# One core's audio layer: constants spread by a product, the row split on GpSimd, the last pair by batch, new engine lists

## What is computed

```
h = conv3(x) + conv_b                          # per channel, over tokens
h = h^T @ lin_w^T + lin_b + mean(emb)          # 250 x 128 per batch
h = layernorm(h) * ln_g + ln_b                 # gamma, beta
n = layernorm(h)
S = (n Wq)(n Wk)^T                             # 250 x 250 per batch
c0 = argmin(rowsum(S[0]))                      # from batch 0 alone
h = h + softmax(S / 8) (n Wv), row c0 zeroed
n = layernorm(h)
out = h + gelu(n tril(W1)^T + b1) tril(W2)^T + b2
```

## Time and profile before

| what | us |
|---|---|
| median of 3 executions | 94.94 (94.71 to 95.37) |
| profiled execution, its own time | 94.69 |
| its span in the trace | 92.9 |
| PE busy | 87.2 |
| DVE busy | 74.4 |
| ACT busy | 69.3 |
| POOL busy | 47.8 |

### The profile page before, as it was taken

How to read it: one execution, slowest core, us unless ns; L and a number is a source line. 1 busy time by engine, 2 the same in 40 slices (tenths; PEclk the granted TensorE clock), 3 DMA queues, 4 the chain that set the end, 5 groups by cost and what they waited for, 6 DMA issues and landing times.

```text
span 92.9 us, 2013 instructions
## 1 busy us (share of the span) xinstructions
PE 87.2 (94%) x567; PEld 73.9 (80%) x567; DVE 74.4 (80%) x296; ACT 69.3 (75%) x215; POOL 47.8 (51%) x70
## 2 busy tenths in 40 slices
PE   4999699999999999999999999999999999999940
PEld 1356567789999999999999999999997877787840
DVE  3279997999698998869998895988989688793560
ACT  1666799899999969977889976697758983565200
POOL 7006398676554386539525519703996305791000
PEclk9999999999999999999999999999999999999999
DMA  2896000000000000000000000000000003036565
GB/s 17 213 280 212 0 0 4 4 0 0 7 0 0 0 0 0 7 4 0 0 4 4 0 7 0 0 0 0 0 0 7 0 0 110 0 110 169 162 175 167
DMA packets 3973, 3.86 MB, mean 42 GB/s; under 512 B 429, under 2 KB 3962, under 8 KB 3962
## 3 DMA queue, kind: packets, MB, share of 16 engines
q1 hardware_dynamic: 3610, 3.35, 12.8%
q10 hardware_dynamic: 352, 0.38, 1.5%
HBM read 1.68 MB, written 2.05 MB: 40 GB/s over the span
## 4 chain that ended last, share of the span: by engine, by line
PE 80%; DVE 9%; DMA 5%; issue 1%; SPq 0%; DVEq 0%
PE bank_o L483 15%; PE bank_s L458 15%; PE bank_at L470 8%; PE bank_pv L434 7%; PE bank_pv L443 7%; PE bank_s L518 7%; DMA x_all<-x_dram 5%; PE bank_x L366 4%; PE bank_x L496 4%; PE bank_nt L507 4%; PE bank_pv L507 4%; PE bank_nt L423 4%; DVE hb_all L1078 2%; DVE tap_a L994 1%; DVE xc L1000 1%; PE bank_o L366 1%
## 5 line engine op out<-in xcount | busy, mean ns | idle before, releaser
L483 PE MATMUL bank_o<-pv,at_sb 125*125 125x129 f32 x128 | 16.8, 273 | 0.0
L458 PE MATMUL bank_s<-n1t,pv 128*125 128x250 f32 x64 | 16.1, 374 | 0.0
L483 PEld LDWEIGHTS bank_o<-pv,at_sb 125*125 125x125 f32 x128 | 15.6, 187 | 0.1
L772 ACT ACTIVATE a<-bank_s,neg_max 125x250 f32<-125x250 f32 x32 | 13.4, 482 | 1.0 <-DVE neg_max L1039 1.0
L1039 DVE TENSOR_REDUCE neg_max<-bank_s 125x2 f32<-125x500 f32 x16 | 10.7, 668 | 2.2 <-PE bank_s L458 2.1
L458 PEld LDWEIGHTS bank_s<-n1t,pv 128*125 128x125 f32 x64 | 11.0, 187 | 0.9
L780 ACT ACTIVATE at_sb<-bank_at 125x500 f32<-125x500 f32 x16 | 9.6, 597 | 2.4 <-PE bank_at L470 1.8
L276 POOL TENSOR_TENSOR hb_all<-h_all,rows_sb 125x512 f32<-125x512 f32 x8 | 10.9, 1384 | 0.0
L765 ACT ACTIVATE pv<-bank_pv 128x508 f32<-128x508 f32 x15 | 9.0, 602 | 2.1 <-PE bank_pv L443 2.0
L272 POOL TENSOR_TENSOR h_all<-h_all,rows_sb 125x512 f32<-125x512 f32 x6 | 7.6, 1271 | 5.7 <-DVE h_all L1013 5.7
L1050 DVE SCALAR_TENSOR_TENSOR h_all<-bank_o,rinv_keep,h_all 125x128 f32<-125x128 f32 x32 | 9.8, 346 | 0.6
(11 more groups left out here) (137 smaller groups left out, 183.7 us busy)
## 6 DMA issues: line engine op xcount, KB each, us to landing
out_dram<-hb_all SPq DMA_DIRECT2D x7, 224.0 KB
x_all<-x_dram SPq DMA_DIRECT2D x8, 125.0 KB, 4.9
out_dram<-hb_all SPq DMA_DIRECT2D x2, 112.0 KB
w_sb<-weights_dram SPq DMA_DIRECT2D x1, 192.0 KB, 5.6
rows_sb<-rows_dram ACTq DMA_DIRECT2D x1, 187.5 KB
out_dram<-hb_all SPq DMA_DIRECT2D x6, 26.0 KB
tok_w<-tok_dram ACTq DMA_DIRECT2D x1, 130.0 KB, 3.1
w_sb<-weights_dram SPq DMA_DIRECT2D x1, 128.5 KB, 5.2
```

Source lines behind the costliest of these rows:

```text
L458: last = nc.tensor.matmul(s_ps[b % 2][:, a, :], p_sb(b)[:, a * H:(a + 1) * H], n1t[b % 2][:, :], start=True, stop=True)
L483: last = nc.tensor.matmul(o_ps[:, a, 0:DV], at_sb[:, c, a * H:(a + 1) * H], v_sb(b, c), start=(c == 0), stop=(c == 1))
L772: last = nc.scalar.activation(a_sb[b % 2][:, a, :], s_ps[b % 2][:, a, :], ACT.Exp, bias=neg_max[b % 2][:, a:a + 1])
```

## The change

- Gamma and beta arrive as one row of 256 numbers in partition 0 of `rows_raw`, whose other partitions POOL has set to zero. A product with `mean_w` (all of whose entries in partition 0 are 1/64) spreads the row over 125 partitions in `bank_at`, and ACT copies it to `rows_sb` times 64 (`spread_constants`, `out_constants`). `wv_centre`, `scale_x(0)` and `add_beta` wait for that copy.
- b2 is a broadcast transfer of its own at the end of SP's loads.
- The constant row is copied from PSUM by ACT over 128 partitions (`out_cb`). POOL splits it in four steps, and `shares_b` (1/32 and 1/64) takes the place of `ones_b`. DVE's six steps go away.
- Pair 1's first tap is ACT's. Three of the nine `keep_warm` products go.
- Pair 7's feed-forward is in two turns (7 and 8), one per batch, from the roots to the output.
- All lists are reordered. In ACT's new list `gelu(0)` stands ahead of `exps(15)`.

```diff
+            sp.dma_start(b2_sb[:, :], rows[:, 2 * D:3 * D].broadcast_to((H, D))).then_inc(landed_b2, 16)
...
+            sp.wait_ge(y_ready, NP + 1)
+            sp.dma_start(out_pairs[NP - 1][0:WIDE, 1], hb_rows[0:WIDE, NP - 1, 1]).then_inc(out_done, 16)
...
+            def split_hi():
+                pool.wait_ge(cb_out, 1)
+                pool.tensor_copy(cb_rows[:, :], cb_sb[:, :]).then_inc(cb_hi_ready, 1)
+            def split_rest():
+                pool.tensor_tensor(cb_rest[:, :], cb_sb[0:64, :], cb_rows[0:64, :], ALU.subtract).then_inc(cb_rest_ready, 1)
+            def split_mid():
+                pool.tensor_copy(cb_rows[0:64, :], cb_rest[:, :]).then_inc(cb_mid_ready, 1)
+            def split_low():
+                pool.tensor_tensor(cb_rows[0:32, :], cb_rest[0:32, :], cb_rows[0:32, :], ALU.subtract)\
+                    .then_inc(cb_ready, 1)
...
             head_root_x(0, 0, 2)
+            split_hi()
+            split_rest()
+            split_mid()
             head_root_x(0, 1, 2)
+            split_low()
...
+            def spread_constants():
+                pe.wait_ge(mean_w_ready, 2)
+                pe.wait_ge(landed_rows, 16)
+                nc.tensor.matmul(bank_at[0:H, 0:2 * D], mean_w[:, 0:H], rows_raw[:, :], start=True, stop=True).then_inc(rows_mm, 1)
...
-            keep_warm(9)
+            keep_warm(6)
+            spread_constants()
             project_first(0)
+            qk_product()
             bias_row()
...
+            def out_constants():
+                act.wait_ge(rows_mm, 1)
+                nc.scalar.activation(rows_sb[:, :], bank_at[0:H, 0:2 * D], ACT.Copy, scale=float(C)).then_inc(rows_out, 1)
+            def out_cb():
+                act.wait_ge(cb_mm, 1)
+                nc.scalar.activation(cb_sb[:, :], bank_s[0][:, 0:D], ACT.Copy).then_inc(cb_out, 1)
...
-            act.dma_start(rows_sb[:, :], rows.broadcast_to((H, 3 * D))).then_inc(landed_rows, 16)
+            act.wait_ge(raw_zeroed, 1)
+            act.dma_start(rows_raw[0:1, :], rows[:, 0:2 * D]).then_inc(landed_rows, 16)
```

More of the change, by code:

```diff
@@ L258, in shared_root, with second_root @@
                     .then_inc(root_ready, 1)
[L260 to L266, removed]
-                    .then_inc(root2_ready, 1)
+            def second_root(n, first, count):
+                cols = slice(first, first + count)
+                pool.wait_ge(stats2, (first + count) // 2)
+                pool.tensor_tensor(ve_2[:, cols], mv_2[:, cols, 1], eps[:, 0:count], ALU.add).then_inc(ve2_ready, 1)
+                pool.wait_ge(ve2_ready, n)
+                pool.tensor_tensor(root_2[:, cols], ve_2[:, cols], neg_half[:, 0:count], ALU.pow)\
+                    .then_inc(root2_ready, 1)
@@ L494, in turn_n2 @@
                     pe.wait_ge(n2t_ready, j - 1)
-                for n in range(4):
-                    last = nc.tensor.transpose(t2_ps[j % 2][:, n * H:(n + 1) * H], n2[:, j, n, :], ident[0:H, 0:H])
+                k, first, count, _ = turn(j)
+                for n in range(count):
+                    last = nc.tensor.transpose(t2_ps[j % 2][:, n * H:(n + 1) * H], n2[:, k, first + n, :], ident[0:H, 0:H])
                 last.then_inc(t2_mm, 1)
@@ L506, in up, with down @@
                     pe.wait_ge(gelu_ready, j - 1)
[L507 to L515, removed]
+                k, first, count, _ = turn(j)
+                nc.tensor.matmul(f1_ps[j % 2][:, 0:count * H], w1_c[:, :], n2t[:, k, first * H:(first + count) * H],
+                                 start=True, stop=True).then_inc(f1_mm, 1)
+            def down(j):
+                k, first, count, _ = turn(j)
+                pe.wait_ge(gelu_ready, j + 1)
+                if 2 <= j <= NP - 1:
+                    pe.wait_ge(y_ready, j - 1)
                 for n in range(count):
                     col = (first + n) * H
-                    last = nc.tensor.matmul(dst[:, n, :], g_sb[:, j, col:col + H], w2_t, start=True, stop=True)
+                    last = nc.tensor.matmul(y_ps[j][:, n, :], g_sb[:, k, col:col + H], w2_t, start=True, stop=True)
                 last.then_inc(y_mm, 1)
[L521 to L525, removed]
             pe.wait_ge(warm_ready, 2)
-            keep_warm(9)
-            pe.wait_ge(mean_w_ready, 2)
-            pe.wait_ge(emb_centred, 1)
+            keep_warm(6)
+            spread_constants()
             project_first(0)
+            qk_product()
             bias_row()
@@ L561, in _ @@
             values(2)
+            project_half(4, 1)
+            turn_a(0)
             turn_n1(3)
+            scores(2)
             project_bias(5)
             project_half(5, 0)
-            project_half(5, 1)
-            turn_a(0)
-            scores(2)
             queries(3)
-            turn_n1(4)
             values(3)
             attend(0)
-            turn_a(1)
+            turn_n1(4)
             scores(3)
             queries(4)
+            turn_a(1)
             turn_n1(5)
+            project_half(5, 1)
             values(4)
@@ L579, in _ @@
             scores(4)
+            queries(5)
             turn_n1(6)
-            queries(5)
             values(5)
@@ L782, in out_n2t @@
             def out_n2t(j):
+                k, first, count, _ = turn(j)
                 act.wait_ge(t2_mm, j + 1)
-                nc.scalar.activation(n2t[:, j, :], t2_ps[j % 2], ACT.Copy).then_inc(n2t_ready, 1)
+                nc.scalar.activation(n2t[:, k, first * H:(first + count) * H], t2_ps[j % 2][:, 0:count * H], ACT.Copy)\
+                    .then_inc(n2t_ready, 1)
             def gelu(j):
+                k, first, count, _ = turn(j)
                 act.wait_ge(f1_mm, j + 1)
-                nc.scalar.activation(g_sb[:, j, :], f1_ps[j % 2], ACT.Gelu, bias=b1_col).then_inc(gelu_ready, 1)
+                nc.scalar.activation(g_sb[:, k, first * H:(first + count) * H], f1_ps[j % 2][:, 0:count * H], ACT.Gelu, bias=b1_col)\
+                    .then_inc(gelu_ready, 1)
             act.wait_ge(landed_tok, 16)
@@ L912, in _ @@
             out_at(14)
-            gelu(0)
             out_n2t(2)
+            gelu(1)
+            gelu(2)
             out_n2t(3)
-            gelu(1)
+            gelu(3)
+            out_n2t(4)
             out_at(15)
-            gelu(2)
-            out_n2t(4)
-            gelu(3)
             out_n2t(5)
+            gelu(4)
             out_n2t(6)
-            gelu(4)
             gelu(5)
```

471 lines of the change are left out of this document (232 added, 239 removed).

## The result

| | median, us | lowest to highest | runs |
|---|---|---|---|
| before | 94.94 | 94.34 to 95.38 | 7 |
| changed | 96.59 | 96.52 to 99.11 | 7 |

The ratio is 1.018, with an interval of 1.014 to 1.023: slower by 1.7 us (96.59 - 94.94), where I had forecast 0.5. That is +1.65 and +1.7.

What follows compares the result with a forecast made beforehand. PE was taken to bound the kernel, busy without a real break from 13.50 to 88.26 us. Head 0, middle 0, table load +1.1 and end -0.6 gave +0.5 on 94.94: 95.4 us, eight in ten from 94.0 to 96.7.

Steps and rivals of the forecast that it cites:

- The likeliest case: Whole kernel: the forecast itself, 95.4 us for the median, own range 94.8 to 96.0, chance 0.48.
- the wide range: Whole kernel: eight chances in ten that the time lies from 94.0 to 96.7 us.
- rival (b): Head and middle: stops from POOL's splits or a late row, cb_ready after about 11.5 us; 96.4 us, chance 0.2.
- (c): Head: the clock rises some 3 us late with six warm-up products, about +1.2 us; 96.6 us, chance 0.06.
- Table load: First feed-forward turns: three loads instead of one, up(1) waits for out_n2t(1); +1.1 us, bounds 0 and +1.7.
- Head: Before the dense stretch: earlier loads gain nothing as roots and splits follow; 0 us, bounds -0.4 and +0.8.
- One of my own signs: Head: the forecast is wrong if PE's first full-rate product comes after 5.2 us.
- Middle: Dense stretch: PE's work per batch untouched, only a few small stops possible; 0 us, bounds 0 and +0.8.
- PE's holes at the end: Last products: down(7) waits about 0.25 us for a Gelu, about 0.3 before; equal, 0 us.
- The end: Output transfers: 0.45 us from less queueing, the rest from ACT's queue; -0.6 us, bounds -0.8 and 0.
- (a): Table loads are free and the head is 0.3 us better; 94.0 to 94.3 us, chance 0.22.
- (d): Feed-forward start: each table switch holds ACT idle for as long again as its 1.28 us load; 97.9 us, chance 0.04.

Runs made afterwards that it cites:

- a_same: The changed kernel run once more, nothing altered, for a profile of an execution of common length: 96.48 us, ratio 1.016 against the kernel before.
- a_ident: The changed kernel with Identity in place of Gelu, so no table is loaded after the first: 95.16 us, ratio 1.003 against the kernel before.
- a_order: The changed kernel with the lists of PE, ACT and DVE from attend(12) on as before, pair 7 still in two turns: 95.67 us, ratio 1.009.
- b_ident: The kernel before with Identity in place of Gelu, as the control: 95.07 us, ratio 1.002.
- b_tail2: The kernel before with pair 7 in two turns and another order of PE's last products, up(8) ahead of down(6): 95.71 us, ratio 1.008.
- b_tail: The kernel before with pair 7's feed-forward in two turns, last products in the changed kernel's order: 95.06 us, ratio 1.001.
- b_load2: The kernel before with one unused Gelu of one column between out_at(13) and exps(15): 96.92 us, ratio 1.020.
- b_warm6: The kernel before with six keep_warm products instead of nine: 98.09 us; ratio 0.996 from its five lower executions alone.
- a_shift: The changed kernel with eight small memsets in DVE's first idle time, moving its later code: 96.52 us, ratio 1.013 against the kernel before.
- a_warm9: The changed kernel with nine keep_warm products instead of six: 96.67 us, ratio 1.019 against the kernel before.
- a_order9: a_order with nine keep_warm products and eight small memsets shifting DVE's code: 95.59 us, ratio 1.006 against the kernel before.
- b_rows: The kernel before with the single gamma/beta row, spreading product, late b2 and seven warm-up products, split still on DVE: 95.09 us, ratio 1.001.

## Why the prediction came out as it did

The direction, the place and the mechanism of the main cost were right; the sum was 1.2 us short. The likeliest case, 95.4 with its own range up to 96.0, did not hold, and neither did the likeliest class: I gave 0.52 to a change within 1%, and it is 1.8%. The measured time is inside the wide range by luck, as rival (b), which did not happen, had stretched it, and (c) lay at 96.6. Term by term, with the profile of `a_same`:

- **Table load, +1.1 forecast, 1.3 measured.** Three loads, `up(1)` held by `n2t`, the third load hidden: all as walked. By starts, as the walk counts, `up(1)` comes 1.20 us late beside `a_ident` instead of 1.1 (the 1.03 of the bracket is the idle time alone), and the product behind it 0.10 more. Taking away the loads gives 1.3 us by the times too, and one Gelu put into the kernel before moves `up(1)` by 1.5.
- **Head, 0 forecast, +0.2 measured.** `attend(12)` starts at 66.71 against 66.93 before, but there `turn_n2(1)` (0.43) was already done, so like is compared with like at 66.50. In `a_order`, where PE has done the same work as before by then, `attend(13)` starts at 70.19 against 69.96. These are single executions, and the head varies between them: in three other profiles with the head of before, the dense stretch begins at 13.41, 13.53 and 13.70 (`b_ident`, `b_tail2`, `b_tail`). So the 0.2 is a reading of two profiles and no more. In `a_same` the dense stretch begins at 13.41, 0.1 earlier than before, and then `queries(0)` waits 0.38 for ACT's `qk_w`, a copy that ACT's longer head list pushed back. I had put that at "as late as before within 0.1", but it starts at 14.93 where it started at 14.47. A copy that ACT reaches at 14.4 and that takes 0.3 could not have released it at 14.47. By 66 us 0.2 of it are left. POOL's splitting steps were near my values, except one of 0.50 where I had taken 0.3. In order of time, POOL in `a_same`:

```profile
8.55 0.28 POOL L277 CAST cb_rows<-cb_sb 128x128 bf16<-128x128 f32 x1
8.92 0.42 POOL L281 TENSOR_TENSOR cb_rest<-cb_sb,cb_rows 64x128 f32<-64x128 f32 x1
9.40 0.50 POOL L285 CAST cb_rows<-cb_rest 64x128 bf16<-64x128 f32 x1
10.14 0.70 POOL L240 TENSOR_TENSOR root_head<-ve_head,neg_half 125x2 f32<-125x2 f32 x1
10.81 0.42 POOL L289 TENSOR_TENSOR cb_rows<-cb_rest,cb_rows 32x128 bf16<-32x128 f32 x1
```

  Batch 1's root ends at 10.84, where I had said 10.6, and pair 2's bias product starts at 11.37, where I had said 11.0. One of my own signs was met here: PE's first product at full rate was to come by 5.2, and in `a_same` it comes at 5.60. It costs nothing by itself, since the same product started at 5.64 before. And the full clock that I read for the whole of the earlier trace rows is not there before 4.5 us: the page's row prints 9 in those slices as well (last section).
- **Middle, 0 forecast, 0 measured.** No hole stands between 18 and 66 us that would not be there before.
- **PE's holes at the end, 0 forecast, +0.1 measured** (0.40 us together against 0.31).
- **The end, -0.6 forecast, about 0 measured.** This is the step that failed. Two things are in it. The transfers give 0.3 (2.6 us from the last `finish` to the end instead of 2.9), not 0.6. The 0.45 that I had for the queueing, the difference between 2.0 and 1.55 us, came true for the bytes (by the packed trace the last packet ends 1.74 us after the last `finish` instead of 2.19), but the landing came only 0.32 earlier (2.22 instead of 2.53). The rest of the 0.6, for ACT's queue, stood on no row and did not come. `b_tail` and `b_tail2` show that the turn by batch alone does not even bring the 0.3. And the last `finish` starts 0.36 late, which no row of before could show.

Together: 0.2 + 1.3 + 0.1 + 0.35 - 0.3 = 1.65 us, which is what the profiled execution lost. Of these, only the table loads are shown by experiments; the others are read from one profile each, and their sum fits no better than such readings can.

The rivals. (a), free loads, is refuted by `a_ident` with its control `b_ident`, and by `b_load2`. (b) named the size nearly, 96.4, but for the wrong reason: `cb_ready` came at 11.2, before its 11.5, and the head costs 0.2. (c), a late clock, exists. I priced it at +1.2 and in the changed kernel it costs 2.5 (99.04 against 96.59) to 3.0 (99.48 against 96.48). It does not make the median of the changed kernel, but 3 of its 13 executions pay it. (d), a switch that costs a second load's time in waiting, is refuted: each of the three loads is followed by its function within 0.02 us. The drain that the Trainium skill ("ScalarE: Activation LUTs", What ACT_TABLE_LOAD costs) adds, about 1.38 us a switch, is in none of these rows. By the Trainium skill (the same title, Table sets: the hidden batching unit), all of one set's functions come before the next, and here the measurement agrees: breaking that order cost 1.3 us.

## What to carry to other kernels

Before you interleave two stages on ACT, write down the function of every instruction in the new list and count the changes: an early Gelu among Exps buys nothing by starting early if PE's next product waits behind the load that brings Exp back, and it is cheap to test by replacing the function. Price a gain at the end of a kernel from the end alone, as a kernel of its own; here, with the transfers' engines no longer full, 2.6 us of the 2.9 stayed. Products that only warm the clock can't be judged by the median of a few executions, as what they buy is how often it rises late.

## What the runs showed of the hardware

- The trace records when the granted clock rises to the full level. In six profiles with six warm-up products it rose at 4.24, 4.52, 5.23 and 5.86 us (`b_warm6`, `a_order`, `a_same`, `a_ident`) and at 13.62 and 13.88 (the 99.04 us execution, `a_shift`), with nothing between. In seven with nine products it rose at 4.50, 4.58, 5.12, 5.55 and 5.64 (`before`, `a_warm9`, `b_ident`, `b_tail2`, `b_tail`), at 7.05 (`a_order9`) and at 14.07 (`b_load2`). The page's clock row prints 9 in the slices ahead of the rise too; the duration of the products shows it.
- The last `finish` starts 0.36 us late in four kernels with one position of DVE's code, and at once when eight instructions are put in front of it.
- A kernel has its own time outside the span. In ten of the twelve kernels of the table the median of time less span is 1.71 to 1.86 us; in `a_order` it is 2.08 and in `b_tail2` 2.49. Each differs from a kernel at 1.7 to 1.8 in the order of lists alone. A span that shrinks is therefore no proof of a shorter time. The pages hold one thing that goes with it, the number of blocks of instructions (16 KB each) fetched within the span. First `a_same`, then `a_order`, whose row `b_tail2` has as well:

```profile
q8 instruction: 5, 0.08, 0.4%
```

```profile
q8 instruction: 4, 0.07, 0.3%
```

  In the kernels with four, the fifth block is fetched after the span, 1.2 us after its end in `a_order` and 1.7 in `b_tail2`. But `b_rows` and `b_warm6` have four as well, the fifth 1.0 us after the span, and spend only 1.84 and 1.86 outside. So the late fetch is a candidate for the lost time and not a cause shown.
